# Cross-attention and packed feed-forward on one core: x of three pairs of slices transposed by 32x32 blocks on VectorE by way of DRAM, and another order of the projection's first blocks

## The reference, cut to what matters

```python
# x, ctx: (8, 256, 1024) f32; Wq, Wk: (1024, 1024)
Q = layernorm(x) @ Wq.T + bq
K = ctx @ Wk.T + bk
attn = softmax(Q @ K.T / sqrt(1024))
x = x + attn @ ctx
weights = scales[g_idx] * (wbin - zeros[g_idx])      # wbin = +1 / -1 from 4-bit weights
x = x + layernorm(x) @ weights + bias
```

## Time and profile before

| | us |
|---|---|
| median of 3 runs | 594.2 |
| the three runs | 593.0, 594.2, 597.47 |
| the profiled execution | 592.89 |
| its span | 591.1 |

### The profile page before, as it was taken

How to read it: one execution, slowest core, us unless ns; L and a number is a source line. 1 busy time by engine, 2 the same in 40 slices (tenths; PEclk the granted TensorE clock), 3 DMA queues, 4 the chain that set the end, 5 groups by cost and what they waited for, 6 DMA issues and landing times.

```text
span 591.1 us, 7737 instructions
## 1 busy us (share of the span) xinstructions
PE 577.9 (98%) x2894; PEld 478.9 (81%) x2894; DVE 378.8 (64%) x621; ACT 215.3 (36%) x408; POOL 188.3 (32%) x135
## 2 busy tenths in 40 slices
PE   8979999999999999999999999999999999999997
PEld 6857888877877877787889899988778888888886
DVE  4896874389678757956103555585896777768442
ACT  6756433301332331332236666655222132122210
POOL 2090000000000000000114977776757624733630
PEclk9989999999999999999999999999999999999999
DMA  7752100040191441505406599997303312310111
GB/s 233 205 211 79 36 1 0 1 142 1 72 317 40 177 177 38 196 18 214 177 3 248 216 333 353 315 416 287 145 2 142 143 71 72 143 72 1 71 72 71
DMA packets 30869, 81.44 MB, mean 138 GB/s; under 512 B 2617, under 2 KB 10817, under 8 KB 28657
## 3 DMA queue, kind: packets, MB, share of 16 engines
q1 hardware_dynamic: 30832, 80.96, 38.2%
HBM read 53.69 MB, written 27.26 MB: 137 GB/s over the span
## 4 chain that ended last, share of the span: by engine, by line
PE 80%; DVE 10%; ACT 3%; DMA 3%; issue 2%; SPq 1%; POOL 0%; DVEq 0%; ACTq 0%
PE bank L1075 21%; PE bank L1077 21%; PE bank L1076 21%; PE bank L1120 3%; PE bank L1126 3%; PE bank L1123 3%; PE bank L1086 2%; DMA wk_stage<-in_L_xattn_Wk 2%; PE bank L1246 2%; PE bank L1176 2%; DVE stats L777 2%; DVE wacc L757 1%; DMA xin<-in_x 1%; DVE wq_lo L721 1%; ACT wq_bk L530 1%
## 5 line engine op out<-in xcount | busy, mean ns | idle before, releaser
L1075 PE MATMUL bank<-xT_hi,m_hi 128*128 128x512 f32 x256 | 105.3, 411 | 0.0
L1077 PE MATMUL bank<-xT_hi,m_lo 128*128 128x512 f32 x256 | 101.0, 394 | 0.0
L1076 PE MATMUL bank<-xT_lo,m_hi 128*128 128x512 f32 x256 | 100.7, 393 | 0.0
L450 POOL TENSOR_TENSOR pairs<-mv,pairs 128x2 f32<-128x2 f32 x16 | 11.1, 695 | 190.9 <-DVE mv L782 190.3
L1029 DVE TENSOR_TENSOR xres<-xres,bank 128x512 f32<-128x512 f32 x56 | 38.4, 686 | 46.2 <-PE bank L1077 46.1
L481 POOL TENSOR_TENSOR l_lo_s<-l_sum_s,l_hi_s 128x512 fp32r<-128x512 f32 x32 | 42.4, 1357 | 71.2 <-DVE l_sum_s L965 71.2
L644 ACT ACTIVATE t_pair<-bank,ucol 128x512 f32<-128x512 f32 x32 | 22.0, 688 | 117.7 <-PE bank L1077 117.7
L467 POOL TENSOR_TENSOR tT_lo<-t_pair,tT_hi 128x1024 fp32r<-128x1024 f32 x16 | 39.2, 2463 | 68.1 <-ACT tT_hi L506 68.1
L1075 PEld LDWEIGHTS bank<-xT_hi,m_hi 128*128 128x128 f32 x256 | 48.2, 188 | 12.0 <-issue 0.2
L1120 PE MATMUL bank<-wk_hi,wq_hi 128*128 128x512 f32 x128 | 52.2, 408 | 5.5 <-DVE wq_lo L721 4.9
L1077 PEld LDWEIGHTS bank<-xT_hi,m_lo 128*128 128x128 f32 x256 | 48.1, 188 | 11.3
(11 more groups left out here) (137 smaller groups left out, 1297.3 us busy)
## 6 DMA issues: line engine op xcount, KB each, us to landing
xin<-in_x SPq DMA_DIRECT2D x8, 1024.0 KB, 6.3
cin<-in_ctx SPq DMA_DIRECT2D x8, 1024.0 KB, 5.7
xres<-in_x SPq DMA_DIRECT2D x8, 1024.0 KB, 11.2
out<-xres SPq DMA_DIRECT2D x15, 512.0 KB, 2.7
right_scratch<-part_hi SPq DMA_DIRECT2D x28, 256.0 KB, 2.2
r_tile<-right_scratch SPq DMA_DIRECT2D x6, 1024.0 KB, 11.2
r_tile<-right_scratch SPq DMA_DIRECT2D x3, 1536.0 KB, 10.4
right_scratch<-part_lo_t SPq DMA_DIRECT2D x16, 256.0 KB, 2.1
```

Of the source, the lines that this page charges most:

```text
L1075: pe.matmul(out_, a_hi, b_hi, start=start, stop=False, skip_group_check=True)
L1076: pe.matmul(out_, a_hi, b_lo, start=False, stop=False, skip_group_check=True)
L1077: return pe.matmul(out_, a_lo, b_hi, start=False, stop=stop, skip_group_check=True)
```

## The change

**x of pairs 1 to 3.** TensorE no longer transposes them; `X_TR` goes, and 96 of its transposes (pair 0's 32 stay). In place of them: slice b of x (b = 2 to 7) is loaded raw into `xin[:, 0]`, normalised into `xin[:, 1]` with its columns dealt to four groups (a column k*128 + a*32 + i goes to a*256 + k*32 + i), stored to DRAM (`xn_scratch`), and loaded again by four DMAs so that group a of the columns lies on partitions 32a to 32a + 31 (`xq[p]`, 16 KB a partition). One VectorE instruction a slice then transposes the 32x32 blocks in place (`x_blocks`, 2048 columns). `x_hi` and `x_lo` of pairs 1 to 3 read `xq` instead of PSUM. The row terms of slices 2 to 7 read `xin[:, 1]` and a second copy of `wrow` in the same column order, which ScalarE writes.

**Order in the pair stage.** Statistics stand at j = 1 and 3, normalising and row terms at j = 2 and 4, block transposes at j = 5 and 6 (both at 6 in pair 2).

**First blocks.** Wq block 2 is loaded ahead of Wk slice 5; its first half is split right behind Wk slice 7; the products and sums with bk come behind instead of ahead of the second halves, one block later; GpSimd's tables wait for the second low half of block 2.

```diff
+    xn_dram = nc.dram_tensor("xn_scratch", [B, S, D], F32).ap()
+        xq = [None] + [at(f"xq{p}", kb, [P, 2 * NB, S], F32) for p, kb in ((1, slot[2]), (2, slot[4]), (3, 162.25))]
-        wrow = at("wrow", 178.25, [P, D], F32)
-        uacc = wrow
+        wrow = at("wrow", 82, [P, D], F32)
+        uacc = at("uacc", 178.25, [P, D], F32)
+        wrow_q = uacc
+        def by_quadrant(rows):
+            return rows.rearrange("q (a k i) -> q k a i", a=4, k=NB)
-        X_TR = {}
...
@@ SyncE
+                if c == 5:
+                    load_wq(2)
                 if c >= 4:
...
-            load_wq(2)
+            def load_raw(b):
+                if b == 2:
+                    sp.wait_ge(s_xtr, NB)
+                    sp.wait_ge(s_dot, 1)
+                else:
+                    sp.wait_ge(s_xn, QT * b)
+                sp.dma_start(xin[:, 0, :, :], x_rows[b]).then_inc(s_xraw, 16)
+            def store_xn(b):
+                sp.wait_ge(s_xn, QT * (b + 1))
+                sp.dma_start(xn_dram[b].rearrange("(t p) f -> p t f", p=P), xin[:, 1, :, :]).then_inc(s_xst, 16)
+            def load_quadrants(b):
+                sp.wait_ge(s_xst, 16 * (b - 1))
...
+                rows = xn_dram[b].rearrange("(m j) f -> j m f", j=32)
+                for a in range(4):
+                    sp.dma_start(xq[b // 2][32 * a:32 * a + 32, b % 2 * NB:(b % 2 + 1) * NB, :],
+                                 rows[:, :, a * S:(a + 1) * S]).then_inc(s_xql[b % 2], 16)
+            load_raw(2)
...
-                    if j == 1 and p + 1 < PAIRS:
-                        sp.wait_ge(s_xtr, NB * (p + 1))
-                        for bt in range(2):
-                            sp.wait_ge(s_dot, 2 * p + bt + 1)
-                            sp.dma_start(xin[:, bt, :, :], x_rows[2 * p + 2 + bt]).then_inc(s_xl[bt], 16)
+                    if p < PAIRS - 1:
+                        if j in (2, 4):
+                            store_xn(2 * p + 1 + j // 2)
+                            if 2 * p + 2 + j // 2 < B:
+                                load_raw(2 * p + 2 + j // 2)
+                        if j == 3 and p < PAIRS - 2:
+                            load_quadrants(2 * p + 2)
+                        if j == 5:
+                            if p == PAIRS - 2:
+                                load_quadrants(2 * p + 2)
+                            load_quadrants(2 * p + 3)
@@ GpSimd
             pool.wait_ge(s_tab[1], 16 * len(QUADRANTS))
+            pool.wait_ge(s_wqlo, wq_split_count(2, 1))
@@ ScalarE
+                if c == NB - 1:
+                    wq_split(2, 0)
...
+                copy(by_quadrant(wrow_q)[:, KH * h:KH * (h + 1), :, :],
+                     bank[4 + h][:, :].rearrange("q (k a i) -> q k a i", k=KH, a=4)).then_inc(s_wrow, 1)
@@ VectorE
+            def x_blocks(b):
+                dve.wait_ge(s_xql[b % 2], 64 * (b // 2))
+                tile = xq[b // 2][:, b % 2 * NB:(b % 2 + 1) * NB, :].rearrange("p m f -> p (m f)")
+                dve.transpose(tile, tile).then_inc(s_xT, 1)
...
             for b in range(NB):
-                if b != 1 and b + 1 < NB:
-                    wq_split(max(b + 1, 2), 0)
+                if 1 < b < NB - 1:
+                    wq_split(b + 1, 0)
...
-                if b != 1 and b + 1 < NB:
-                    wq_split(max(b + 1, 2), 1)
-                if b != 1 and b + 1 < NB:
-                    sum_bk(b + 1 if b > 1 else 0)
+                if b == 0:
+                    wq_split(2, 1)
+                    sum_bk(0)
+                elif 1 < b < NB - 1:
+                    sum_bk(b)
+                    wq_split(b + 1, 1)
...
-                        if j in (2, 3):
-                            x_stats(2 * p + j)
-                            x_apply(2 * p + j)
-                        if j in (4, 5):
-                            row_terms(2 * p - 2 + j)
+                        if j in (1, 3):
+                            x_stats(2 * p + 2 + j // 2)
+                        if j in (2, 4):
+                            x_apply(2 * p + 1 + j // 2)
+                            row_terms(2 * p + 1 + j // 2)
+                        if j == 5 and p < PAIRS - 2:
+                            x_blocks(2 * p + 2)
+                        if j == 6:
+                            if p == PAIRS - 2:
+                                x_blocks(2 * p + 2)
+                            x_blocks(2 * p + 3)
@@ TensorE
-                        for u in X_TR.get((p, j, i), ()):
-                            x_tr(p + (j > 0), u)
```

More of the change, by code:

```diff
@@ L196, in xattn_ffn_kernel @@
         s_stat, s_rstd, s_xn, s_dot = sem("ln_stats"), sem("ln_rstd"), sem("xn_done"), sem("row_terms")
+        s_xraw, s_xst = sem("x_of_later_pairs_loaded"), sem("xn_stored")
+        s_xql = [sem(f"xn_reloaded{i}") for i in range(2)]
+        s_xT = sem("xn_transposed_by_blocks")
         s_xtr, s_xhi, s_xlo = sem("xn_transposed"), sem("xT_hi_done"), sem("xT_lo_done")
@@ L579, in _ @@
                 act.wait_ge(s_wr, h + 1)
-                copy(wrow[:, h * HALF:(h + 1) * HALF], bank[4 + h][:, :]).then_inc(s_wrow, 1)
+                copy(wrow[:, h * HALF:(h + 1) * HALF], bank[4 + h][:, :])
+                copy(by_quadrant(wrow_q)[:, KH * h:KH * (h + 1), :, :],
+                     bank[4 + h][:, :].rearrange("q (k a i) -> q k a i", k=KH, a=4)).then_inc(s_wrow, 1)
             def c_hi(b, u):
@@ L782, in ln_stats @@
                 dve.tensor_scalar(mv[:, :, 1], mv[:, :, 1], EPS, None, ALU.add).then_inc(s_stat, 1)
-            def ln_apply(buf, n, done):
-                dve.wait_ge(s_rstd, n + 1)
-                for t in range(QT):
-                    dve.tensor_scalar(buf[:, t, :], buf[:, t, :], mv[:, t, 0:1], rstd[:, t:t + 1],
-                                      ALU.subtract, ALU.mult).then_inc(done, 1)
-            def x_stats(b):
-                dve.wait_ge(s_xl[b % 2], 16 * (b // 2 + 1))
-                ln_stats(xin[:, b % 2, :, :])
@@ L794, in x_apply, with x_stats @@
-            def x_apply(b):
-                ln_apply(xin[:, b % 2, :, :], b, s_xn)
+            def x_stats(b):
+                if b < 2:
+                    dve.wait_ge(s_xl[b], 16)
+                    ln_stats(xin[:, b, :, :])
+                else:
+                    dve.wait_ge(s_xraw, 16 * (b - 1))
+                    ln_stats(xin[:, 0, :, :])
+            def x_apply(b):
+                dve.wait_ge(s_rstd, b + 1)
+                if b == 2:
+                    dve.wait_ge(s_xtr, NB)
+                elif b > 2:
+                    dve.wait_ge(s_xst, 16 * (b - 2))
+                for t in range(QT):
+                    if b < 2:
+                        out_, in_ = xin[:, b, t, :], xin[:, b, t, :]
+                    else:
+                        out_, in_ = by_quadrant(xin[:, 1, t, :]), xin[:, 0, t, :].rearrange("q (k a i) -> q k a i", k=NB, a=4)
+                    dve.tensor_scalar(out_, in_, mv[:, t, 0:1], rstd[:, t:t + 1], ALU.subtract, ALU.mult).then_inc(s_xn, 1)
@@ L797, in x_lo @@
+            def x_blocks(b):
+                dve.wait_ge(s_xql[b % 2], 64 * (b // 2))
+                tile = xq[b // 2][:, b % 2 * NB:(b % 2 + 1) * NB, :].rearrange("p m f -> p (m f)")
+                dve.transpose(tile, tile).then_inc(s_xT, 1)
             def x_lo(p, u):
                 dve.wait_ge(s_xhi, NB * p + u + 1)
-                low(xT_lo[:, u, :], bank[6 + u % 2][:, :], xT_hi[:, u, :], s_xlo)
+                if p == 0:
+                    low(xT_lo[:, u, :], bank[6 + u % 2][:, :], xT_hi[:, u, :], s_xlo)
+                else:
+                    low(xT_lo[:, u, :].rearrange("p (m j) -> p m j", j=32), xq[p][:, :, 32 * u:32 * u + 32],
+                        xT_hi[:, u, :].rearrange("p (m j) -> p m j", j=32), s_xlo)
@@ L822, in _ @@
                     sum_bk(1)
-                    sum_bk(2)
+                if b == NB - 2:
+                    sum_bk(NB - 1)
             x_lo(0, 6)
@@ L839, in row_terms @@
                         i = QT * b + t
-                        order.link(dve.tensor_tensor_reduce(junk, xin[:, b % 2, t, cols], wrow[:, cols], 1.0, 0.0,
-                                                            ALU.mult, ALU.add, cdot[:, h, i:i + 1]))
+                        order.link(dve.tensor_tensor_reduce(junk, xin[:, min(b, 1), t, cols], (wrow if b < 2 else wrow_q)[:, cols],
+                                                            1.0, 0.0, ALU.mult, ALU.add, cdot[:, h, i:i + 1]))
                 cols = slice(QT * b, QT * (b + 1))
@@ L1077, in three, with x_tr @@
                 return pe.matmul(out_, a_lo, b_hi, start=False, stop=stop, skip_group_check=True)
-            def x_tr(p, u):
-                g = NB * p + u
-                pe.wait_ge(s_xn, 4 * p + 4)
-                wait(pe, s_xlo, g - 1)
+            def x_tr(u):
+                pe.wait_ge(s_xn, 4)
+                wait(pe, s_xlo, u - 1)
                 for bt in range(2):
```

40 lines of the change are left out of this document (22 added, 18 removed).

## The result

The changed kernel takes 605.2 us (median of 4 runs, 604.4 to 608.6) where the kernel before takes 595.8 (4 runs, 593.0 to 597.5): ratio 1.017, 95% interval 1.011 to 1.023. Forecast were 585 and 576 to 596. The profiled execution took 605.4 us, its span is 603.6.

A forecast was written before the change was run, and what follows sets the result against it. TensorE, busy 577.9 of 591.1 us, was taken as the bound, each new wait paid in full. Profiled execution 592.9-6.4-10.4+7.5 = 583.6; the median shown is 1.3 above that execution, so about 585; range 576 to 596, likeliest case 580 to 589.

The forecast's parts named there:

- First blocks, -6.4: Projection's first blocks: TensorE's stops and slow steps, 6.66 us, nearly all go with the new order; sum -6.4 us.
- the second `wq_lo` wait: Projection: TensorE's stop from 47.20 to 48.43, 1.23 us, behind VectorE's low half of Wq; +0.2 expected to remain.
- Transposes removed, -10.4: Pair stage: 12 groups of eight x transposes leave TensorE, 0.87 us each, nothing covering them; -10.4 us.
- Prices on VectorE: VectorE's added work: six block transposes at 2.3 us each; twelve normalising operations stay at 809 ns.
- Rival A: VectorE in the pairs is dearer: transpose 3.9, normalise 1.33 us; 598 us in all; chance 0.15 (590 to 600).
- New waits, +7.5: Pair stage: TensorE's new waits for VectorE, +6.4 in pair 0, +1.1 in pair 1, 0 in pair 2.
- the walk along VectorE's queue: Pair stage: VectorE's in-order queue followed on the old time axis to get the new waits, +7.5 us.
- The trip, 4 + 6 to 7 us: Normalised x through DRAM ahead of each block transpose: 4 us for the store, 6 to 7 for the reload.
- Rival B: Each pair's second transpose waits for a late store and reload, 7 us more a trip; 604 us; chance 0.10.
- Rival E: TensorE's granted clock falls after new stops, unhidden: two times 1.7 us, 588; counted within the forecast's 0.56.
- The signs it named: Pair stage: VectorE 95% busy in pair 0; reloads that VectorE waits for by over 5 us would refute the prediction.

The follow-up runs named there:

- front_only: The kernel before with only the new order of the projection's first blocks; x of every pair still transposed on TensorE; 587.0 us, ratio 0.989.
- blocks_only: The changed kernel with the old order of the projection's first blocks, so only the way by VectorE and DRAM is changed; 611.8 us, ratio 1.032.
- no_row_terms: The changed kernel without the row terms' four products per slice of x for slices 2 to 7, waits kept; 604.8 us, ratio 1.019.
- weights_first: The changed kernel with SyncE issuing the stores of the weights' halves ahead of x's stores and loads at each pair-stage step; 598.4 us, ratio 1.008.
- step_earlier: weights_first with row terms one step later and, in pairs 1 and 2, x's steps one earlier, next raw load behind reloads; 591.5 us, ratio 0.996.

## Why the prediction was wrong, point by point

- **First blocks, -6.4: right.** front_only 6.4 us (interval 4.1 to 8.7). Two things are not as told. A wait for `wk_lo` of 2.0 us, before 31 us, is new in the trace of after; but it varies between executions whatever the order. Where Wk's loads landed in 3.7 to 4.5 us (median) it is 0.6 to 1.8, where they took 5.3 to 5.9 it is 1.8 to 2.9, and the kernel before is of the first kind, blocks_only, with the old order, of the second. Like with like, the stage starts 5.9 and 6.5 us sooner. And the second `wq_lo` wait is not always gone: 1.4 us in front_only, none in after.
- **Transposes removed, -10.4: right** where no stop hides it (3.45 a pair).
- **Prices on VectorE: right.** Block transpose forecast 2.3, measured 2.27 to 2.31; normalising forecast 0.81, measured 0.806 to 0.815 in all sixteen operations, twelve of them in the new order. The rule of the Trainium skill, Vector Engine (DVE) Microarchitecture Reference, Measured stream behaviour on trn2, under which the price stays, fits these numbers. Rival A falls with them, and no_row_terms takes the rest of it away.
- **New waits, +7.5: wrong, 21.4.** Pair 0 came in below its 6.4, at 3.7: the gather 2.85, from 128.9 on (forecast 3.1 near 128), 0.85 for `xT_lo` (forecast 2.1), and the smaller waits of 1.0 and 0.4 did not come. Pair 1 was put at 1.1 and is 1.46+7.45; pair 2 at 0 and is 8.72. The failed step is the walk along VectorE's queue in these pairs. It followed VectorE, and x's own transfers, and took every other engine as ready. It never walked SP's queue with what was *moved behind* the new requests there, the 56 stores of the weights' halves, nor ScalarE's two buffers, which make a late store a wait of ScalarE, VectorE and TensorE in turn. weights_first shows some 5 of the 18 us to lie there. The rest is the length and the start of the trip, next.
- **The trip, 4 + 6 to 7 us: too short where it counts.** Medians in the changed kernel: store 4.9, reload 6.2. The raw load of batch 3, put at 6.9, took 7.5 to 7.7 behind the store. The reload's 6.2 is of one request; the four of a slice took 11.3 us in pair 1 of weights_first, and the whole trip 16.6 where the prediction had 11.3 (196.7 to 208). In weights_first VectorE waited up to 5.5 us for a reload. step_earlier takes no work away and wins 13 us against the changed kernel (by ratio): it moves the weights' stores, the trips, the raw loads and VectorE's steps for x, and nothing else.
- **Rival B ended nearest** (604, chance 0.10). Half of its mechanism is shown: the trips are late. Its evidence against itself was the error: the queues' share of 0.19 to 0.43 was read from the kernel *before*, and the change itself raises it to 0.55 to 0.73. It had only the transfers' length, not the order in which others stand behind them.
- **Rival E, the clock:** priced as two times 1.7 us and left out of the sum of 585; it was three times, 7.6 us in all. It belongs to every long new stop: each of the three waits of 2.85 us or more was followed by about 6 us at 0.51 to 0.63.
- **The signs it named:** VectorE waits 0.5 us for reloads in the changed kernel, below the 5 named, only because it stands still for the high halves instead; it is 87% busy in pair 0 (45.27 of 52.21 us between the first and the ninth eviction), not 95%.
- **Range:** 576 to 596 was too narrow since both ends were built from prices of single operations, which were right on VectorE, and not from the schedule.

## What to carry to other kernels

When a change adds DMA requests to a queue, write down for each queue what now stands behind the new ones and which engine needs it, and price it with the DMA share that the change will cause, not the one it finds. Put a wait for x's transfers behind work that other engines wait for, on VectorE and on the issuing queue alike; it was the timetable, and at the end two more buffers, not the work, that decided between 605 and 586 us. And count TensorE's stops one and a fifth to one and a third times: 7.6 us went to the lower clock here beside 21.4 of stops, and in the other kernels of the table with the way by DRAM the stage is longer by 0.18 to 0.34 of the stops than work and stops alone make it.
